# A decoder layer on one core: the second feed-forward product in three fp32r terms, and a written-out start and end of every engine's program

## The reference, cut to what matters

```python
x = _layernorm(x + mamba2(x, ...))          # 16 heads of 16 channels, state size 64, causal over 1024 rows
x = _layernorm(x + cross_attention(x, ctx_1024, mask, ...))   # 16 heads, 77 context rows, masked softmax
h = relu(einsum('bsh,hi->bsi', x, W1) + b1)                   # 256 -> 1024
x = _layernorm(x + einsum('bsi,ih->bsh', h, W2) + b2)         # 1024 -> 256
```

## Time and profile before

| what | value |
|---|---|
| median of three runs | 738.28 us |
| profiled execution | 738.45 us, span 736.7 us |
| PE busy | 688.5 us (93%) |
| DVE busy | 509.0 us (69%) |
| ACT busy | 488.4 us (66%) |
| POOL busy | 332.8 us (45%) |
| mean granted TensorE clock | 0.991 |
| DMA queue 1 | 8.6% of 16 engines |

### The profile page before, as it was taken

How to read it: one execution, slowest core, us unless ns; L and a number is a source line. 1 busy time by engine, 2 the same in 40 slices (tenths; PEclk the granted TensorE clock), 3 DMA queues, 4 the chain that set the end, 5 groups by cost and what they waited for, 6 DMA issues and landing times.

```text
span 736.7 us, 21679 instructions
## 1 busy us (share of the span) xinstructions
PE 688.5 (93%) x8522; PEld 589.9 (80%) x8522; DVE 509.0 (69%) x1264; ACT 488.4 (66%) x1234; POOL 332.8 (45%) x606
## 2 busy tenths in 40 slices
PE   4687889999999999999999999999999999999997
PEld 3466767878888888878888788888888888898896
DVE  2337788767676867767686776768687676778742
ACT  4578587966858685785958577685867768351532
POOL 1113646544553644455463446446344535544341
PEclk9999799999999999999999999999999999999999
DMA  5611000000101010010001000000101000000000
GB/s 152 215 11 40 10 25 10 24 11 9 31 11 31 17 32 17 9 31 10 31 17 32 17 18 24 9 30 18 31 18 31 17 3 16 17 16 9 16 16 28
DMA packets 24432, 20.44 MB, mean 28 GB/s; under 512 B 8511, under 2 KB 23180, under 8 KB 24076
## 3 DMA queue, kind: packets, MB, share of 16 engines
q1 hardware_dynamic: 24332, 19.06, 8.6%
HBM read 14.02 MB, written 4.19 MB: 25 GB/s over the span
## 4 chain that ended last, share of the span: by engine, by line
PE 77%; ACT 13%; DVE 4%; issue 4%; POOL 0%; DMA 0%; SPq 0%; POOLq 0%; DVEq 0%; ACTq 0%
PE bank L514 15%; PE bank L504 12%; PE bank L348 8%; PE bank L292 5%; PE bank L461 4%; PE bank L409 4%; ACT E L646 4%; PE bank L484 4%; PE bank L429 4%; PE bank L362 3%; PE bank L335 2%; ACT L601 2%; PE bank L304 2%; ACT L646 2%; PE bank L276 2%
## 5 line engine op out<-in xcount | busy, mean ns | idle before, releaser
L1050 POOL TENSOR_SCALAR st<-st 128x1 f32<-128x1 f32 x96 | 21.4, 223 | 270.7 <-DVE st L888 270.7
L514 PE MATMUL bank<-w,hT 128*128 128x256 f32 x512 | 116.2, 380 | 0.0
L1081 POOL TENSOR_TENSOR P<-P,rc 128x308 f32<-128x308 f32 x128 | 89.3, 729 | 44.8 <-DVE rc L952 44.8
L514 PEld LDWEIGHTS bank<-w,hT 128*128 128x128 f32 x512 | 94.9, 190 | 11.8 <-issue 0.2
L646 ACT ACTIVATE E<-bank 128x512 f32<-128x512 f32 x128 | 67.8, 600 | 35.5 <-PE bank L335 35.3
L834 DVE TENSOR_TENSOR E<-bank,E 128x512 f32<-128x512 f32 x128 | 81.3, 677 | 4.3 <-POOL E L1041 3.2
L348 PE MATMUL bank<-Cc,Bc 64*128 64x128 f32 x1024 | 75.3, 286 | 7.0 <-ACT E L646 2.4
L1041 POOL TENSOR_SCALAR_AFFINE_SELECT E<-E 128x508 f32<-128x508 f32 x128 | 80.1, 649 | 0.0
L348 PEld LDWEIGHTS bank<-Cc,Bc 64*128 64x128 f32 x1024 | 63.5, 189 | 19.9 <-issue 8.6
L716 ACT ACTIVATE hT<-bank,b1c 128x256 f32<-128x256 f32 x128 | 58.5, 487 | 29.3 <-PE bank L504 28.5
L939 DVE TENSOR_REDUCE mx<-bank 128x4 f32<-128x308 f32 x128 | 60.1, 470 | 10.2 <-PE bank L447 9.3
(11 more groups left out here) (108 smaller groups left out, 1631.9 us busy)
## 6 DMA issues: line engine op xcount, KB each, us to landing
xT<-in_xT SPq DMA_DIRECT2D x16, 256.0 KB, 3.1
xr<-in_x SPq DMA_DIRECT2D x32, 128.0 KB, 2.1
out<-res SPq DMA_DIRECT2D x32, 128.0 KB, 1.7
RB<-DL SPq DMA_DIRECT2D x128, 4.0 KB
w<-in_w SPq DMA_DIRECT2D x1, 1024.0 KB, 7.7
hT<-in_w SPq DMA_DIRECT2D x1, 1024.0 KB, 10.3
PT<-in_kvw SPq DMA_DIRECT2D x1, 512.0 KB
P<-in_ctxT SPq DMA_DIRECT2D x1, 308.0 KB
```

The source lines that it names most:

```text
L514: i = eng.matmul(bk[:, 0:256], hT[:, m, cols(n)], w2[:, m, :], start=m == 0, stop=m == 7)
L1081: eng.tensor_tensor(v, v, rc[:, n % 2, 4 * j:4 * j + 4].unsqueeze(2).to_broadcast([128, 4, S]), ALU.mult).then_inc(p_norm, 1)
```

## The change

Three things are changed.

First, `ffn2` multiplies in three fp32r terms. W2 is split once into `w2h` and `w2l`, each hidden block into `hh` and `hl`, and each of the eight steps of the sum is three matmuls in place of one. For the split, ACT now writes relu into a small tile `hr` with room for four blocks (two pairs), POOL copies a pair to fp32r (`h_hi`, new), and DVE subtracts to get the rest (`h_low`, new). Relu of a pair waits until `h_low` has read the pair two before it. Second, W1 and W2 are loaded in four pieces of 512 KB through `hr` (`load_w`), and POOL splits each piece (`split_w`, new); DVE's `start_w1` goes. Third, `PAIRS` goes: on every engine the first and the last four periods are written out call by call in an order of their own, and a loop of some 13 periods stands between. The order inside the middle periods is also another than before. To make room, `la`, `tT`, `qT` and `oT` have one buffer in place of two, with their waits moved by one tile, and the mask row `mr` holds half as much and is read twice.

```diff
-        w2 = sb("w2", [128, 8, 256])
+        w2h = sb("w2h", [128, 8, 256], R)
+        w2l = sb("w2l", [128, 8, 256], R)
-        hT = sb("hT", [128, 8, GW])
+        hr = sb("hr", [128, 2, 2, GW])
+        hh = sb("hh", [128, 8, GW], R)
+        hl = sb("hl", [128, 8, GW], R)
 # PE, ffn2(n)
+                pe.wait_ge(w_lo, 4)
                 for m in range(8):
-                    pe.wait_ge(relu, 8 * (n // GT) + m + 1)
-                    i = eng.matmul(bk[:, 0:256], hT[:, m, cols(n)], w2[:, m, :], start=m == 0, stop=m == 7)
+                    pe.wait_ge(h_rest, 4 * (n // GT) + m // 2 + 1)
+                    for k, (hm, wm) in enumerate(((hh, w2h), (hh, w2l), (hl, w2h))):
+                        i = eng.matmul(bk[:, 0:256], hm[:, m, cols(n)], wm[:, m, :], start=m == 0 and k == 0,
+                                       stop=m == 7 and k == 2)
 # ACT, hidden(g, ms)
-                act.wait_ge(ffn2_mm, GT * g)
+                act.wait_ge(w_lo, 4)
                 for m in ms:
+                    act.wait_ge(h_rest, 4 * g + m // 2 - 1)
                     act.wait_ge(ffn1_mm, 8 * g + m + 1)
-                    eng.activation(hT[:, m, :], b_ffn1[g, m][:, 0:GW], ACT.Relu, ...)
+                    eng.activation(hr[:, m // 2 % 2, m % 2, :], b_ffn1[g, m][:, 0:GW], ACT.Relu, ...)
 # DVE, new
+            def h_low(g, j):
+                dve.wait_ge(ffn2_mm, GT * g)
+                dve.wait_ge(h_top, 4 * g + j + 1)
+                eng.tensor_tensor(hl[:, 2 * j:2 * j + 2, :], hr[:, j % 2, :, :], hh[:, 2 * j:2 * j + 2, :].bitcast(F),
+                                  ALU.subtract).then_inc(h_rest, 1)
 # POOL, new
+            def split_w(c):
+                pool.wait_ge(ld_w1, DMA * (c + 1))
+                dst = ...                      # piece c of w1h, w1l (c < 2) or of w2h, w2l
+                eng.tensor_copy(dst[0], wraw).then_inc(w_hi, 1)
+                pool.wait_ge(w_hi, c + 1)
+                eng.tensor_tensor(dst[1], wraw, dst[0].bitcast(F), ALU.subtract).then_inc(w_lo, 1)
+            def h_hi(g, j):
+                pool.wait_ge(ffn2_mm, GT * g)
+                pool.wait_ge(relu, 8 * g + 2 * j + 2)
+                eng.tensor_copy(hh[:, 2 * j:2 * j + 2, :], hr[:, j % 2, :, :]).then_inc(h_top, 1)
 # SP, new
+            def load_w(c):
+                sp.wait_ge(w_lo, c)
+                eng.dma_start(wraw, src).then_inc(ld_w1, DMA)
```

PE's order at the start was `tok(0)`, `cum(0)`, `bc(0, 0)`, `tok(1)`, `bc(0, 1)`, `cum(1)`, `diff(0, 0)`, `gmat(0, 0)`, `diff(0, 1)`, `tok(2)`, `cum(2)`, `keys_values()`. It is now:

```diff
+            tok(0)
+            bc(0, 0)
+            cum(0)
+            bc(0, 1)
+            tok(1)
+            tok(2)
+            cum(1)
+            diff(0, 0)
+            diff(0, 1)
+            gmat(0, 0)
+            ecum(1)
+            cum(2)
+            diff(1, 0)
+            bc(1, 0)
+            keys_values()
+            bc(1, 1)
+            state_in(0)
+            gmat(0, 1)
+            gmat(1, 0)
+            diff(1, 1)
+            y(0)
...
+            for s in range(4, 17):
+                gmat(2 * s - 3, 0)
+                query(2 * s - 5)
+                out_proj(2 * s - 4)
+                state_turn(2 * s - 4)
+                cum(2 * s - 1)
+                diff(2 * s - 2, 0)
+                score(2 * s - 5)
+                ffn2(2 * s - 10)
+                p_turn(2 * s - 6)
...
+                ffn1(s - 4, range(3, 6))
+                gmat(2 * s - 2, 1)
+                state_in(2 * s - 2)
+                pv(2 * s - 5)
+                ffn1(s - 4, range(6, 8))
...
+            attn_proj(31)
+            x2_turn(30)
+            ffn2(28)
+            x2_turn(31)
+            ffn2(29)
+            ffn1(15, range(0, 3))
+            ffn1(15, range(3, 6))
+            ffn1(15, range(6, 8))
+            ffn2(30)
+            ffn2(31)
```

More of the change, by code:

```diff
@@ L39 @@
 KD = 10
-PAIRS = range(-1, NG + 6)
 def blk_rows(m):
@@ new lines, in _ @@
+            tok(3)
+            state_in(1)
+            inter(1)
+            y(1)
+            state_turn(1)
+            gate(1)
+            state_in(2)
+            x1_turn(0)
+            cum(3)
+            tok(4)
+            query(0)
+            bc(2, 0)
+            score(0)
+            out_proj(1)
+            cum(4)
+            tok(5)
+            ecum(3)
+            gmat(2, 0)
+            gmat(2, 1)
+            state_turn(2)
+            diff(3, 0)
+            bc(2, 1)
+            x1_turn(1)
@@ new lines, in _ @@
+            y(2)
+            inter(2)
+            gate(2)
+            query(1)
+            out_proj(2)
+            p_turn(0)
+            diff(3, 1)
+            score(1)
+            inter(3)
+            diff(4, 0)
+            gmat(3, 0)
+            state_in(3)
+            diff(4, 1)
+            gmat(3, 1)
+            ecum(4)
+            cum(5)
+            tok(6)
+            pv(0)
+            y(3)
+            gate(3)
+            x1_turn(2)
+            state_turn(3)
+            bc(3, 0)
@@ L563, in _ @@
                 gate(2 * s - 3)
+                ecum(2 * s - 1)
+                cum(2 * s)
                 attn_proj(2 * s - 6)
                 query(2 * s - 4)
[L566 to L572, removed]
-                score(2 * s - 4)
-                out_proj(2 * s - 3)
-                ffn1(s - 4, range(0, 3))
@@ L585, in _ @@
+                tok(2 * s + 1)
+                x1_turn(2 * s - 3)
                 inter(2 * s - 2)
+                y(2 * s - 2)
+                attn_proj(2 * s - 5)
+                gate(2 * s - 2)
+                x2_turn(2 * s - 6)
+                bc(s, 1)
+            query(29)
+            gmat(31, 0)
+            out_proj(30)
+            state_turn(30)
+            score(29)
+            gmat(31, 1)
+            ffn2(24)
+            p_turn(28)
+            x2_turn(27)
+            ffn2(25)
@@ new lines, in _ @@
+            pv(28)
+            y(31)
+            inter(31)
+            gate(31)
+            x1_turn(30)
+            attn_proj(28)
+            ffn1(13, range(0, 3))
+            query(30)
+            p_turn(29)
+            out_proj(31)
+            score(30)
+            pv(29)
+            ffn1(13, range(3, 6))
+            x1_turn(31)
+            ffn1(13, range(6, 8))
+            query(31)
+            attn_proj(29)
+            x2_turn(28)
+            score(31)
+            ffn2(26)
@@ new lines, in _ @@
+            p_turn(30)
+            x2_turn(29)
+            ffn2(27)
+            ffn1(14, range(0, 3))
+            pv(30)
+            ffn1(14, range(3, 6))
+            p_turn(31)
+            attn_proj(30)
+            pv(31)
+            ffn1(14, range(6, 8))
+            attn_proj(31)
[7 more added lines that the diff above has]
+            ffn2(30)
```

594 lines of the change are left out of this document (455 added, 139 removed).

## The result

The kernel after takes 709.73 us in the median of four runs (708.94 to 710.94), the kernel before beside it 737.79 us (736.99 to 738.47). The ratio is 0.9622, with a 95% interval of 0.9604 to 0.9639: 28 us less. The profiled execution took 709.73 us with a span of 708.0 us. The forecast was 714.5 us.

The account below looks back on a forecast made before the run. PE was taken as the bound in the middle and end. From 738.45 us: product -18.3, new waits +4, start -10, end +0.5, giving 714.6, or 714.5 as median; forecast 707 to 720 us, range 702 to 729.

Parts of the forecast that it names:

- What bounds the kernel: PE bounds middle and end, idle 1.17 us of a 43.0 us period; the start holds 47 us of loss.
- Part 1: ffn2 on PE: three fp32r products for one fp32 product, 2.87 for 3.46 us a tile, 18.3 us less in all.
- Part 2: Hidden-block splits on DVE and POOL: 0.3 us more PE idle time on each of 13 periods, 4 us.
- The collision on the port: h_low and POOL instructions shut each other out: half of 64 h_low wait about 0.35 us, 0.5 us a period on DVE.
- Part 3: Start: the new order fills holes and W1's split moves to POOL, 10 us less; bounds 0 to 23 us.
- that sentence of the prediction: Start: SP's residual loads and rows stand behind waits for a piece's split, which are short against POOL's order.
- Part 4: End and small edits: PE has no holes to fill, the last hidden block adds 0.5 us, bounds 0 to 3.
- A (the hidden path): Middle: PE waits for h_low's result or what stands behind it, period stays 43.0 us, 725 us in all; chance 0.18.
- B (DVE as pacemaker): Middle: DVE cannot close its idle time, periods above 44.0 us, middle case 744.6 us, slower; chance 0.09.
- C (start only ACT's): Start: the explicit order closes nearly all holes, 20 us instead of 10, 704 us in all; chance 0.17.
- D: ffn2 on PE: three products no cheaper than one, at 0.144 us or more a matmul, 732 us; chance 0.04.

Follow-up runs that it names:

- experiment 3: The changed kernel without the third term of the product, 704.91 us; then also without the subtraction h_low, 698.11 us.
- experiment 1: The changed kernel with plain fp32 ffn2 back and no split of the hidden blocks, new order of calls kept: 723.37 us.
- two_terms_no_low: The changed kernel without the third term (low part of hidden block times high part of W2) and without the subtraction h_low: 698.11 us.
- experiment 7: The changed kernel with its start in the loop's order: 738.04 us; V stack put behind row copies too: 737.88 us; load_w also behind them: 725.0 us.
- experiment 6: The changed kernel with its end not written out, the middle loop running on to period 22: 709.9 us.
- order_alone: The kernel of experiment 1: the changed kernel with plain fp32 ffn2 back, new order of calls kept, 723.37 us.
- experiment 4: The changed kernel with each h_low subtraction made twice on DVE: 748.99 us.
- experiment 2: The changed kernel's three-term product and splits put into the old order of calls: 809.78 us; with casts and subtractions at other places: 748.03 us.
- rows_early: The changed kernel with row copies of tiles 3 and 4 issued inside the V stack on SP's queue: 706.04 us.
- two_terms: The changed kernel without the third term (low part of hidden block times high part of W2), all splits kept: 704.91 us.
- loop_end: The kernel of experiment 6: the changed kernel with its end in the loop's order, 709.9 us.

## Why the prediction was right, step by step

**What bounds the kernel.** Right in the middle and the end. What the windows of before couldn't show is the ring of experiment 3, a floor of 41 us under a period of 41.5.

**Part 1, the product.** Forecast 0.57 us a tile, 1.14 a period; 1.16 a period was measured between the kernel with the old and that with the new product. Two errors cancel in this: a call cost 3.02 us, not 2.87, and the fp32 call that it replaces cost 3.65 in the new order, not 3.46. Against before as it stood (3.46 and 3.51 us for the two calls of a period) the new ones (3.02 and 3.05) save 0.9 us a period by these pieces of the chain, and 1.1 us from start to start.

**Part 2, the new waits: the term that was mis-sized.** The prediction added 0.3 us of idle time to each of 13 periods, 4 us. There is none on balance: PE's idle time is 0.44 us a period where 1.2 to 1.8 was forecast, because the order took 0.83 us of it away (experiment 1) and the product put 0.1 back. I charged the splits for their waits and gave the new order nothing in the middle, where 1.17 us of idle time lay open in the earlier trace rows. For the twelve periods the sum had 13.7 - 3.7 = 10.0 us, the runs 17.1: 3.2 us from the order, and 3.9 more from the product, which came to 13.9 us with its waits where the sum had 13.7 without them. That is 7.1 us too little; the start (0.6 us) and the end (1.6 us) missed the other way, and the sum is off by 4.8. So the range was met in part because errors of both signs cancel. The durations: `h_low` 0.724 us (0.83 forecast), `h_hi` 0.624 (0.65), a split on POOL 1.04 + 2.36 = 3.4 us (4.2). DVE is busy 33.3 us in a period, below the 34 to 35 of the forecast.

**The collision on the port.** `h_low` has a median of 679 ns, a mean of 724 and a longest of 1216. POOL's `decay` takes 656 ns without the subtraction (two_terms_no_low), 691 in after, 703 with it done twice; `soft_norm` 703, 739 and 784. So DVE and POOL do hold one another up, as the Trainium skill (SBUF — State Buffer, the part on the shared port pair) has it for two SBUF inputs. The price on DVE was smaller than my 0.35 us for half of the subtractions (0.18 us each): taken as the mean less the median it is 64 x 0.045 = 2.9 us in all, an estimate. On POOL it is 4.4 us in `decay` and 4.8 in `soft_norm` against the kernel without the subtraction, 0.14 us for each subtraction, near the 0.18 forecast.

**Part 3, the start.** 10 us forecast, 9.4 measured in the profiled execution, out of two terms that I had not kept apart: the order 13.1 and the product -3.7, of which only 1 us stands in an execution with the clock up. That the two together fall so near to 10 is luck. `y(0)` came at 38.53 us (36 to 43 forecast), the first `ffn1` at 120.0 (126 forecast; that sum left out that the new order has 6.9 us less other work ahead of it). In the written order SP did stand for a split (from 65.8 to 81.2 us), and PE didn't wait for rows behind it, so that sentence of the prediction holds in what counts; in the loop's order the same kind of wait costs 13 us (experiment 7).

**Part 4, the end.** For eight tiles and the last group 3.8 us of gain were in the sum (8 x 0.57, less 0.5 and the thirteenth period's 0.3), and 2.2 were measured, all of it the product's. PE's work fell by 3.5 us and its idle time rose by 1.4 us against order_alone, where 0.5 was forecast. That the written end does nothing was in the forecast too (no holes to fill), and experiment 6 shows it.

**The rivals.** A (the hidden path) would show PE waiting for `hl` and periods of 43 us: it waits 0.5 us in the whole span. B (DVE as pacemaker) doesn't happen, but stands close: experiment 4 gets there with 0.75 us more for each `h_low`, and experiment 2 mostly by wrong places. Its reasoning that DVE can close little of its idle time was sound; the product left it just enough. C (start only ACT's) came to 13.1 of its 20 us for the order, but the product took 3.7 back. D is excluded by the chain's 3.02 against 3.65 us (by the prediction's own terms D gives 733 us, not 732).

## What to carry to other kernels

Where a bound engine has idle time in its steady period, ask what an edit that reorders the period can give back of it, and don't only charge it for new waits. Before taking more work off the busiest engine, look for a ring of hand-overs about as long as its work, and whether the work you take off stands on that ring: here one lay right under it, the product stood beside it, and 30 us less work brought 5. A place in a single trace of a start is sure to a few us only; a second trace of the same program tells how much. When PE waits for a small transfer, read the issuing queue from its head: what stands there may be a wait for a third engine, and moving that one instruction was worth 13 us.

## What the runs showed of the hardware that was not expected

- The V stack, 25 small copies from SBUF to SBUF, holds SP's queue for 21.7 us, 0.87 us each, and each set of four row copies for 2.6 to 2.75 us. Nothing behind them is issued meanwhile.
- PE's granted clock fell behind its waits: from 60 to 82 us it is 0.84 in the kernel with the new order alone, where PE waits 3.9 us for the rows of DL, 0.91 in after (2.45 us), 1.00 in rows_early (none). It doesn't follow the length of the wait alone: with the same wait of 3.9 us it is 0.84 in two_terms and 0.92 in loop_end. At the lower level `bc` takes 2.09 us, at the higher 1.15.
- POOL's cast of 128x512 to fp32r takes 0.62 us and of 128x1024 1.04 us, its subtraction of 128x1024 with two SBUF inputs 2.36 us; DVE's of 128x512 0.68 us in the median.
- What eight fp32 matmuls of 128x256 cost from start to start hangs on the call behind them: 3.46 us ahead of `state_turn` and 3.55 to 3.60 ahead of `gmat` in before, 3.56 ahead of `p_turn` and 3.65 ahead of `diff` with the new order. Why isn't shown. The 24 fp32r matmuls of after take 2.92 to 2.96 and 3.01 to 3.05 us in the last two places.
